# Attention inside a decoder layer: 4 KB rows in the DRAM scratch of the query and key stacks, and an earlier query remainder on VectorE

## The reference, cut to what matters

```python
x = layernorm(x + mixer(x))
# attention: 16 heads of 8 channels, 128 queries and 128 keys per sequence
q = split_heads(x @ Wq + bq);  k, v = split_heads(ctx @ Wk + bk), split_heads(ctx @ Wv + bv)
scores = where(mask, -1e15, einsum('bhqd,bhkd->bhqk', q, k) / sqrt(8))
x = layernorm(x + softmax(scores) @ v @ Wo + bo)
x = layernorm(x + experts(x))     # 16 experts, 4 chosen per token, and a shared one
```

## Time and profile before

| | |
|---|---|
| median of 3 runs | 696.97 us (694.66 to 699.02) |
| profiled execution | 701.77 us, span 700.0 us |
| mean granted TensorE clock | 0.947 of full |
| PE busy | 610.4 us (87%) |
| DVE busy | 495.2 us (71%) |
| ACT busy | 256.6 us (37%) |
| POOL busy | 261.2 us (37%) |
| DMA | 40.34 MB, of which q1 (issued by SP) 36.74 MB |

### The profile page before, as it was taken

One profiled execution on the slowest core, in us unless ns is written; L12 is line 12 of the kernel. 1 busy time (PEld: TensorE's weight loads), 2 busy tenths in 40 slices (PEclk: granted clock), 3 DMA queues, 4 the chain that ended last, 5 costly groups with the idle time before them and its releaser, 6 DMA issues. The chain is left out here.

```text
span 700.0 us, 17981 instructions
## 1 busy us (share of the span) xinstructions
PE 610.4 (87%) x6368; PEld 502.8 (72%) x6368; DVE 495.2 (71%) x1246; ACT 256.6 (37%) x444; POOL 261.2 (37%) x301
## 2 busy tenths in 40 slices
PE   6589999999999754888779879779799999999995
PEld 5467778778777553676667767557688888888884
DVE  2877887887887554657567667486578778787873
ACT  2443442443343200635445435335322323332221
POOL 4263754754752575405145144362101101110111
PEclk9989999999999975789999999999999999999998
DMA  6020000000000485275484763800001000000000
GB/s 204 0 62 1 16 15 0 15 15 14 1 16 1 114 200 99 70 142 133 106 159 126 138 132 93 188 6 6 32 0 32 30 0 30 30 0 30 16 16 16
DMA packets 53553, 40.34 MB, mean 58 GB/s; under 512 B 3968, under 2 KB 48288, under 8 KB 53488
## 3 DMA queue, kind: packets, MB, share of 16 engines
q1 hardware_dynamic: 50896, 36.74, 22.2%
q0 software_dynamic: 704, 1.92, 1.2%
q10 hardware_dynamic: 1888, 0.79, 0.6%
HBM read 24.10 MB, written 11.93 MB: 51 GB/s over the span
## 5 line engine op out<-in xcount | busy, mean ns | idle before, releaser
L1917 PE MATMUL bank<-xT_hl_c,w_up 128*128 128x512 f32 x432 | 118.1, 409 | 2.4 <-ACTq L67 2.4
L1244 DVE TENSOR_REDUCE nmax<-bank 128x4 f32<-128x512 f32 x112 | 72.0, 685 | 54.9 <-PE bank L1399 48.3
L141 POOL TENSOR_TENSOR rstd<-mv,norm_c 128x4 f32<-128x4 f32 x24 | 6.4, 267 | 264.3 <-DVE mv L135 251.2
L1151 ACT ACTIVATE prob<-bank 128x512 f32<-128x512 f32 x128 | 69.4, 594 | 67.2 <-PE bank L1399 42.0
L1917 PEld LDWEIGHTS bank<-xT_hl_c,w_up 128*128 128x128 f32 x432 | 76.1, 189 | 15.9 <-ACTq L67 2.7
L1389 PE MATMUL bank<-neg_i,mask 64*128 64x256 bf16 x512 | 54.3, 292 | 36.4 <-issue 9.5
L1839 ACT ACTIVATE sg<-bank 128x512 f32<-128x512 f32 x72 | 43.0, 597 | 105.3 <-PE bank L1917 105.3
L1933 PEld LDWEIGHTS bank<-w_down,hid 128*128 128x128 f32 x576 | 74.4, 191 | 5.9 <-issue 0.5
L738 POOL TENSOR_TENSOR ramp<-upto,dec_hl 128x512 fp32r<-128x512 f32 x64 | 66.8, 1073 | 26.1 <-PE bank L866 26.1
L1933 PE MATMUL bank<-w_down,hid 128*128 128x128 f32 x576 | 75.6, 275 | 0.0
L1872 DVE TENSOR_TENSOR gu<-sg,bank 128x512 f32<-128x512 f32 x64 | 43.8, 685 | 21.5 <-PE bank L1917 10.5
(11 more groups left out here) (227 smaller groups left out, 1265.1 us busy)
## 6 DMA issues: line engine op xcount, KB each, us to landing
q_stack<-q_scratch SPq DMA_DIRECT2D x32, 192.0 KB, 5.4
k_scratch<-k_part SPq DMA_DIRECT2D x8, 384.0 KB, 3.2
q_scratch<-q_part SPq DMA_DIRECT2D x8, 384.0 KB, 2.7
k_stack<-k_scratch SPq DMA_DIRECT2D x32, 96.0 KB
x<-xT_in SPq DMA_DIRECT2D x8, 256.0 KB, 8.3
mask<-mask_in SPq DMA_DIRECT2D x8, 256.0 KB, 6.0
xres<-x_in SPq DMA_DIRECT2D x8, 256.0 KB, 2.8
q_scratch<-q_part SPq DMA_DIRECT2D x8, 256.0 KB, 3.1
```

The source lines that it names most:

```text
L1151: act.activation(prob[:, b % 2, ORDER[n], :, :], (TT0, TT1)[n % 2][:, :], ACT.Exp, scale=XD ** -0.5)\
L1244: dve.tensor_reduce(nmax[:, b, 4 * u:4 * u + 4], (SS0, SS1)[n % 2][:, :].rearrange("p (i k) -> p i k", i=4), AX_X, ALU.max, negate=True).t ...
L1917: mm = pe.matmul(bank[:, :], w_up[:, which, a, c, :], xT_hl[par][:, v, :], start=(n == 0), stop=(n == 2))
```

## The change: what it does

- **Scratch.** q and k scratch both become (2, 2 halves, 4 rows, 128, 256 tokens). A half group is now contiguous, and the eight heads (c) of one channel row lie side by side: 8 x 256 tokens x 2 bytes, a run of 4 KB.
- **Stores.** `store_parts` writes rows for each half by one DMA (three parts, 512-byte runs), and the first part a second time for both halves by a third DMA. Three DMAs and 512 KB for each of q and k; before it was three DMAs and 768 KB for q, one of 384 KB for k. The place of the parts in the key tile changes (`AT`), so that three neighbours and one repeat give the order that both reads need.
- **Reads.** One function `stack` for both: rows 0 to 3 by a DMA of 32 partitions, and rows 4 and 5, which are two neighbours of the four again (`AGAIN`), by one of 16. For a half that is four DMAs for k (before six) and four for q (before two). The stacks get the shape [128, 2 halves, 8, 256], so that a run is 4 KB on this side too.
- **VectorE.** `part_rest` of the query and the maxima of b = 2 move ahead of `statistics`.

```diff
-    a.dram = [nc.dram_tensor(n, (2, rows, P, GT), BF16, kind="Internal").ap() for n, rows in (("q_scratch", NP), ("k_scratch", 3))]
+    a.dram = [nc.dram_tensor(n, (2, 2, KEPT, P, 2 * P), BF16, kind="Internal").ap() for n in ("q_scratch", "k_scratch")]
...
-    if which:
-        sp.dma_start(a.dram[1][par].rearrange("r p t -> p r t"), a.part[1][:, :, :]).then_inc(a.stored[1].sem[par], 16)
-        return
-    for r, n, p in PAIRS:
-        sp.dma_start(a.dram[0][par, r:r + n].rearrange("r p t -> p r t"), bc(a.part[0][:, p, None, :], [P, n, GT]))\
-            .then_inc(a.stored[0].sem[par], 16)
+    part, rows, done = a.part[which], a.dram[which][par], a.stored[which].sem[par]
+    first = 1 - which
+    for half in range(2):
+        tok = slice(half * 2 * P, half * 2 * P + 2 * P)
+        sp.dma_start(rows[half, first:first + 3].rearrange("r p t -> p r t"), part[:, :, tok]).then_inc(done, 16)
+    sp.dma_start(rows[:, 3 * which].rearrange("h p t -> p h t"), part[:, 0, :].rearrange("p (h t) -> p h t", h=2)).then_inc(done, 16)
+
+
+def stack(sp, a, par, half, which, tile):
+
+    rows = a.dram[which][par, half].rearrange("r (e j c) t -> j r e (c t)", e=XD, j=2)
+    again = AGAIN[which]
     for j in range(2):
-        for r, n in ((0, 3), (3, 2), (5, 1)):
-            sp.dma_start(k_stack[64 * j + r * XD:64 * j + (r + n) * XD, :, tok],
-                         rows[j][0:n].rearrange("r e c t -> (r e) c t")[:, :, tok]).then_inc(a.stacked[1][half].sem[par], 16)
...
+        for r, src in ((0, rows[j]), (KEPT, rows[j][again:again + NP - KEPT])):
+            n = (KEPT, NP - KEPT)[r == KEPT]
+            sp.dma_start(tile[64 * j + r * XD:64 * j + (r + n) * XD, half, :, :].rearrange("p c t -> p (c t)"),
+                         src.rearrange("r e x -> (r e) x")).then_inc(a.stacked[which][half].sem[par], 16)
...
                 if left:
                     maxima(g + 1, 1, (2, 3))
                     split_maxima(g + 1, 0)
+                if left >= 2:
+                    part_rest(dve, a, g + 2, 0, PF)
+                if left:
+                    maxima(g + 1, 2)
                 if before:
                     statistics(dve, g - 1, v_res, dve_passed, res, stats, mv)
...
-                if left >= 2:
-                    part_rest(dve, a, g + 2, 0, PF)
...
                 if left:
-                    maxima(g + 1, 2)
                     maxima(g + 1, 3)
```

More of the change, by code:

```diff
@@ L148, in normalise_pool @@
     pool.tensor_tensor(out, res[:, :, :], bc(rstd[:, :, None], [P, GS, P]), ALU.mult).then_inc(done.sem, 1)
-PAIRS = ((0, 3, 0), (3, 2, 1), (5, 1, 2))
-NP = 6
+AT = ((0, 1, 2), (0, 2, 1))
+NP, KEPT = 6, 4
+AGAIN = (1, 2)
 class Projections:
@@ L173, in projection_tensors @@
     a.rest = sb("rest", [P, 2, GT])
[L174 to L176 removed]
+    a.dram = [nc.dram_tensor(n, (2, 2, KEPT, P, 2 * P), BF16, kind="Internal").ap() for n in ("q_scratch", "k_scratch")]
+    a.first = sb("q_stack0", [P, 2, XH // 2, 2 * P], BF16), sb("k_stack0", [P, 2, XH // 2, 2 * P], BF16)
     a.ones = ctx.enter_context(nc.semaphore("k_stack0_ones"))
@@ L183, in projection_tensors @@
     a.act, a.dve, a.third = (sem("q_act", 2), sem("k_act", 2)), (sem("q_rest"), sem("k_rest")), (sem("q_third"), sem("k_third"))
-    a.stored = DmaSem(ctx, nc, "q_stored", 3), DmaSem(ctx, nc, "k_stored", 1)
-    a.stacked = [[DmaSem(ctx, nc, f"{x}_stacked{h}_", n) for h in range(2)] for x, n in (("q", 2), ("k", 6))]
+    a.stored = DmaSem(ctx, nc, "q_stored", 3), DmaSem(ctx, nc, "k_stored", 3)
+    a.stacked = [[DmaSem(ctx, nc, f"{x}_stacked{h}_", n) for h in range(2)] for x, n in (("q", 4), ("k", 4))]
     return a
@@ L221, in part_second @@
     act.wait_ge(a.dve[which].sem, a.dve[which].at(g))
-    act.activation(a.part[which][:, 1, :], a.rest[:, which, :], ACT.Copy).then_inc(a.act[which].sem, 1)
+    act.activation(a.part[which][:, AT[which][1], :], a.rest[:, which, :], ACT.Copy).then_inc(a.act[which].sem, 1)
 def part_rest(dve, a, g, which, bank):
@@ L235, in part_third @@
     pool.wait_ge(a.act[which].sem, a.act[which].at(g, 1))
-    pool.tensor_tensor(a.part[which][:, 2, :], a.rest[:, which, :], a.part[which][:, 1, :], ALU.subtract)\
+    pool.tensor_tensor(a.part[which][:, AT[which][2], :], a.rest[:, which, :], a.part[which][:, AT[which][1], :], ALU.subtract)\
         .then_inc(a.third[which].sem, 1)
@@ L667, in group @@
                     for half in range(2):
-                        stack_k(sp, a, 0, half, a.first[1])
+                        stack(sp, a, 0, half, 1, a.first[1])
                     store_parts(sp, a, 1, 1, 1)
@@ L671, in group @@
                     for half in range(2):
-                        stack_q(sp, a, 0, half, a.first[0])
+                        stack(sp, a, 0, half, 0, a.first[0])
             pairs(sp, group)
@@ L753, in group @@
                 if left == 1:
-                    pool.memset(a.first[1][:, :, :].bitcast(F32), TWO_ONES).then_inc(a.ones, 1)
+                    pool.memset(a.first[1][:, :, :, :].bitcast(F32), TWO_ONES).then_inc(a.ones, 1)
             coefficients(pool, 1)
@@ L983, in attention @@
         xs = sb("xs", [P, 2, GS, P])
-        q_stack, k_stack = ((first, sb(n, [P, XH // 2, GT], BF16)) for first, n in zip(a.first, ("q_stack1", "k_stack1")))
+        q_stack, k_stack = ((first, sb(n, [P, 2, XH // 2, 2 * P], BF16)) for first, n in zip(a.first, ("q_stack1", "k_stack1")))
         v_d = sb("v_d", [P, 2, GS, UNITS * DIAG])
@@ L1044, in stacks @@
                 sp.wait_ge(p_t.sem, p_t.at(g - 2, 8 * half + 7))
-                stack_k(sp, a, par, half, k_stack[par])
+                stack(sp, a, par, half, 1, k_stack[par])
                 sp.wait_ge(a.stored[0].sem[par], a.stored[0].at(g, par))
-                stack_q(sp, a, par, half, q_stack[par])
+                stack(sp, a, par, half, 0, q_stack[par])
             def group(g, par, left):
@@ L1393, in products @@
             def products(banks, left_stack, right_stack, k, par, b, p, done):
-                tok = slice(b * P, (b + 1) * P)
+                half, tok = b // 2, slice(b % 2 * P, b % 2 * P + P)
                 for i in range(4):
@@ L1398, in products @@
                         row, c0 = unit_rows(2 * j + p)
-                        mm = pe.matmul(banks[j][:, i * P:(i + 1) * P], left_stack[par][row:row + k, c0 + i, tok],
-                                       right_stack[par][row:row + k, c0 + i, tok], start=False, stop=True, skip_group_check=True)
+                        mm = pe.matmul(banks[j][:, i * P:(i + 1) * P], left_stack[par][row:row + k, half, c0 + i, tok],
+                                       right_stack[par][row:row + k, half, c0 + i, tok], start=False, stop=True, skip_group_check=True)
                         if i == 3:
```

16 lines of the change are left out of this document (3 added, 13 removed).

## The result

| | before | after |
|---|---|---|
| median of 4 runs each | 698.00 us (694.66 to 701.99) | 679.11 us (677.87 to 679.64) |
| ratio | | 0.9725, 95% interval 0.967 to 0.9779 |
| profiled execution (span) | 701.77 (700.0) | 679.41 (677.7) |
| mean granted TensorE clock | 0.947 | 0.960 |
| PE busy | 610.4 us | 600.6 us |

The kernel is 2.75% faster. A second measurement on another chip gave 0.9707 (0.9673 to 0.974).

The account below looks back on a forecast made before the run. PE, near its limit in each attention round, was held by the stack's store-and-read chain. Gaps -16.0, seventh round -0.8, clock -5.0, start +0.5, new waits +0.8 make -20.5 us: 697.0 to 676.5, so 677 us, range 667 to 691.

Parts of the forecast that it names:

- PE's gaps: PE's attention waits for query stacks (14.3 us) and maxima (4.2 of 6.6 us winnable): 16.0 us of 18.5 would go.
- what comes up: Waits hidden so far, mostly on ACT, that PE meets where it catches up: 0.8 us lost (0 to 5).
- The chain: From first query store to PE's next stack scores: 9.0 us (bounds 7.7 and 11.9) in place of 10.7.
- The clock: PE's granted clock after long stack waits: 5 of 7.0 us given back when no stack wait exceeds 1 us.
- The start: Attention start, where SP issues 22 DMAs where it had 20: 0.5 us lost (-0.3 to 1.5).
- The maxima: Maxima of b = 2 ahead of statistics: PE's 1.03 us wait goes, later statistics cost 0.4; net 0.6 to 0.7 a round.
- The seventh round: PE's 2.41 us wait for the maxima's parts, DVE's casts being slow beside POOL's weight split: 0.8 us won (0 to 2.4).
- the signs named ahead: Profile after: stack waits under 1 us, chain 9.0, clock 1.00, rounds 23 to 24.5 us; wrong if waits return under another engine's name.
- One of the chances: Chance of a time faster than 690 us, given as 0.80 from 0.65 + 0.10 + half of 0.17 and a little more.
- That the reads don't get faster: Rival, chance 0.17: partitions written, not runs, set the stack reads' rate at 180 GB/s; chain 10.2 us, total 689 us.
- The wait that takes the place of another: Rival, chance 0.10: POOL's later norm meets a late ACT, k_proj waits, rounds keep half the gain; 687 us.
- The stores of 512-byte runs: Rival, chance 0.08: the query store lands late, decisive from 8.1 us after first issue, shifting everything behind it; 708 us.

Follow-up runs that it names:

- Run 2: Kernel after with VectorE's old order, so only the new scratch, stores and reads against the kernel before: 682.06 us, ratio 0.976.
- the second execution: Second profiled execution of the unchanged kernel after, from its repeat measurement beside its variants: median 679.78 us, ratio 0.9707 to the kernel before.
- Run 4: Kernel after with the second half's four reads of query stack 0 moved to the start of SP's attention program: 679.88 us, ratio 0.972.
- run 12: Kernel after with the maxima of b = 2 behind the statistics again, only the query remainder ahead of them: 677.51 us, ratio 0.968.
- run 1: Kernel before with VectorE's new order alone (query remainder and maxima of b = 2 ahead of the statistics): 692.91 us, ratio 0.992.
- Run 9: Kernel after with POOL's split of the expert weights moved right behind their load: 674.61 us, ratio 0.9629.
- Run 3: Kernel after with the stacks shaped as before, so reads land in runs of 512 bytes: 683.90 us, ratio 0.9784.

## Why the prediction was right

The forecast of 677 us came out at 679.1 for the median, and -20.5 at -22.4 for the profiled execution. Term by term:

- **PE's gaps, right in sum and in what they hung on, but so close by luck.** The sum had -16.0 for stacks and maxima, -0.8 for the seventh round and +0.8 for what comes up: -16.0. The idle time of the attention fell by 16.1. But the stacks gave 12.7 and the maxima 6.0, 18.7 together. Against that stand longer waits for the parts (+3.7), for the maxima's rows in the rounds (+2.3) and for the weights (+1.1), 7.1 where the sum had nothing net. And 3.0 went at the start of the block, 0.9 where the loop goes back and 1.2 in waits for exponentials, which no term had. Small gaps make the rest. Run 2 shows that the stack was what most of the gain hung on.
- **The chain, right in sum, not in its parts.** 9.0 was forecast, 9.3 measured. The reads begin 3.6 us after the first store where I had 4.6: the last store's landing time of 3.5 became 2.5, for 128 KB in both kernels, with fewer bytes ahead of it. The four issues take 2.5 us, where I took 1.4 to the start of the last one (1.9 with it), and PE goes on 3.2 after them, for 2.5 by my sum. The price of 0.48 an issue, read from the key reads, holds for the second half's four, 1.81 or 0.45 each; why the first half's cost 0.62 each no run separates.
- **The clock, too small.** 5.0 was forecast, and PE's busy time in the attention fell by 10.3, or by 6.3 in the second execution. I had looked at the waits for stacks alone. From the stack to the output projection the four long waits gave back 7.1 us, which are the 7.0 of which I took 5: 6.60, 5.33 and 5.30 us became 3.77, and in the sixth round, where this stretch holds fewer matmuls, 3.82 became 2.64:

```profile
450.45 1.52 PE L1470 MATMUL bank<-w_o,ctxT 128*128 128x128 f32 x8
...
424.60 1.16 PE L1464 MATMUL bank<-w_o,ctxT 128*128 128x128 f32 x8
```

  For the rest no run separates a cause. One place stands out: at the start of the block, where the wait of 4.42 us for the maxima's rows fell to 1.45, PE's busy time ahead of it is 11.9 us for 14.0. No run changed the clock by itself, so this split is argued from the windows and not shown.
- **The start, too small, and of no account.** 0.5 was forecast, 2.5 measured. The eight last reads are issued in 4.02 us, 0.50 each, and they stand behind eight key reads and three stores in the queue. Kernels with this same start begin the block between 247.9 and 249.9 us, so a single execution doesn't give the term closely. Run 4 shows that giving it back brings nothing.
- **The maxima, wrong in mechanism.** I had a cost of 0.4 a round for the later statistics and a net gain of 0.6 to 0.7. The row that I read for it was DVE's alone. What it cost was the collision of the maxima's split with POOL's norm, 0.9 to 1.1 us in four rounds, and it took the whole of the gain (run 12; run 1 shows that the wait comes with the order). The earlier trace rows had shown such a cast at 2.27 us instead of 0.18 beside POOL; I used it for the seventh round and not for the others, into which the same change moved POOL's norm.
- **The seventh round.** Its term came as forecast, 2.41 us of waiting for the parts became 1.65 (but 2.27 in the second execution), and still the round got 0.7 us longer between its output projections: a wait of 2.90 for the maxima's rows is new, and behind the round one of 1.10 for the weights. Run 9 takes the latter away and leaves the former (2.81); what makes that one late stays open.
- **The experts** took 1.6 us more, which no term had; they began at a clock of 0.63. The second execution has neither, so this isn't a cost of the change.

The overshoot of 1.9 us on the profiled execution is thus -5.3 for the clock, +2.0 for the start, +1.6 for the experts and -0.1 for the gaps, which makes -1.8; the 0.1 left is rounding. The medians differ by 18.9, since the execution profiled before was slower than its median by 3.8. Of the signs named ahead, two failed in part: two of the six rounds shown are 27.0 and 27.7 us long, not 23 to 24.5, and their clock is 0.94; and waits did come back under another name, 3.7 us for the parts, which the prediction had called a sign of being wrong. One of the chances was added wrongly: 0.65 + 0.10 + half of 0.17 is 0.835, not 0.80.

**The rivals.** That the reads don't get faster failed by its chain, not by its rate: the windows after have 180 GB/s from 320 to 325 us and 199 from 324 to 326, hardly more than before, and yet the chain is 9.3 and not 10.2, for the reads begin 3.6 us after the first store, not 4.9. The DMA share in these windows is 0.63 and 0.65, where it was 1.02 and 1.21, so they hold pauses and don't say how fast the reads could go. Run 3 puts 4 to 5 us on the run's length, at the edge of the noise. The wait that takes the place of another did come, by VectorE's order and not by ACT's; its price was 1.1 a round, and the round as a whole kept its gain. The stores of 512-byte runs had landed by 3.6 us after the first issue, when the query reads begin, not at 8.1.

## What to carry to other kernels

In a chain of store, landing, read and landing, count the issues ahead of the last one and the bytes of the store; here fewer bytes stored and a shorter landing paid for two more reads, and the variant with six stores in place of three cost 9 us. When an operation moves on one engine, look at what its reader on another engine now stands beside: VectorE and GpSimd hold each other up for whole instructions, so a few operations of 0.2 us belong where GpSimd isn't working on SBUF. And where a gain in a loop doesn't show in the total, look for the first in-order wait behind the loop: 7.9 us sat in the wait for one split of weights that had 17 us of idle GpSimd ahead of it, 7 to 8 of them with the weights already there, by run 9. And before a part of a gain is put down to the clock, profile the same kernel twice: here two executions differed by 4.0 us in the busy time of the same matmuls.

## What the runs showed of the hardware

- A VectorE operation on 32 columns beside a GpSimd one ends with it: with two inputs 1.22 and 1.20 us instead of 0.19, a cast 0.51 instead of 0.18. That was known to me for one cast of the seventh round; that it decides what a moved operation is worth, in three places of this kernel, was not. The reductions from PSUM (1.29 for two) took the same with and without it.
- Most groups of DMAs from SP are issued in 0.45 to 0.52 us each, by the kernel after's timeline (four in 1.72 and 1.81, eight in 4.02). The first half's query reads take 0.62 to 0.75 each there (2.50 and 3.01 for four), and 0.89 in 512-byte runs (3.56).
- From 61361 to 39186 packets at the same bytes the landing of 128 KB goes from 3.4 to 2.9 us; the program gets 0.6 to 0.8% shorter, at the edge of the noise.
- While the stacks are read the rate is 180 to 199 GB/s in 4 KB runs (two windows of the kernel after, DMA share 0.63 and 0.65), 169 to 180 in 512-byte runs (DMA share 1.21 and 1.02).
- The same kernel, executed twice, had a granted clock of 0.93 and 0.91 in the attention, and 187.7 and 191.7 us of busy PE for 3901 matmuls.
